# LSTM cell, step size and its product moved to GpSimd, and four buffers for the products with B, in a Mamba stage

## The reference

```python
dt = softplus(einsum('blr,cr->blc', dt_in, dw) + db)      # the step size
def step(h, inp):
    dA = exp(dt_t[..., None] * A)
    h = dA * h + (dt_t * u_t)[..., None] * B_t[:, None, :]
    y = einsum('bcn,bn->bc', h, C_t)
# the LSTM, each direction, 33 time steps of 64 sequences, 64 hidden units
g = xt @ wih.T + h @ whh.T + bih + bhh
i, f, gg, o = split(g, 4)
c = sigmoid(f) * c + sigmoid(i) * tanh(gg)
h = sigmoid(o) * tanh(c)
```

## Time and profile before

| What | Value |
|---|---|
| median of 3 runs | 2159.1 us (2152.12 to 2165.97) |
| profiled execution | span 2159.5 us from its first to its last instruction; it has no other time of its own |
| busy in the span | PE 1857.5, DVE 1645.7, ACT 1298.3, POOL 1011.2 us |
| Mamba and LSTM stage | first scan at 46.3 us, last product with C at 836 us |
| idle time of GpSimd before products with B | 203.4 us over the kernel |
| a load of B, 429 KB | 4.6 us from issue to landing |

### The profile page before, as it was taken

How to read it: one execution, slowest core, us unless ns; L and a number is a source line. 1 busy time by engine, 2 the same in 40 slices (tenths; PEclk the granted TensorE clock), 3 DMA queues, 4 the chain that set the end, 5 groups by cost and what they waited for, 6 DMA issues and landing times. The chain is left out here.

```text
span 2159.5 us, 49411 instructions
## 1 busy us (share of the span) xinstructions
PE 1857.5 (86%) x19547; PEld 1357.8 (63%) x19547; DVE 1645.7 (76%) x2609; ACT 1298.3 (60%) x2660; POOL 1011.2 (47%) x775
## 2 busy tenths in 40 slices
PE   7888888889888867897878878889788699999999
PEld 4444444444443323444568877767676599999999
DVE  4999999999999996678465442346554589999897
ACT  5777777777776645114345444252456388888886
POOL 1777777777777773110017777300440033333333
PEclk9999999999999999899679999898899699999999
DMA  3544444444444442520038889501730411112000
GB/s 130 167 132 132 126 137 132 132 132 127 128 139 140 132 137 55 126 45 1 7 100 236 258 257 256 139 1 73 231 114 12 187 64 64 65 65 69 14 7 7
DMA packets 98037, 241.63 MB, mean 112 GB/s; under 512 B 15024, under 2 KB 48320, under 8 KB 95504
## 3 DMA queue, kind: packets, MB, share of 16 engines
q1 hardware_dynamic: 89120, 218.12, 32.7%
q0 software_dynamic: 7680, 15.74, 3.2%
q10 hardware_dynamic: 1008, 4.62, 0.6%
HBM read 226.25 MB, written 12.19 MB: 110 GB/s over the span
## 5 line engine op out<-in xcount | busy, mean ns | idle before, releaser
L1119 POOL TENSOR_TENSOR dBu<-du,Bs 128x858 f32<-128x858 f32 (+1 forms) x240 | 588.2, 2452 | 203.4 <-DVE hst L1046 94.6
L574 PE MATMUL py<-hst,ident 128*128 128x429 f32 (+1 forms) x960 | 416.7, 565 | 95.9 <-DVE hst L1056 95.1
L1046 DVE TENSOR_TENSOR_SCAN hst<-dA,dBu 128x858 f32<-128x858 f32 (+1 forms) x240 | 457.8, 1908 | 17.1 <-ACT dA L889 13.7
L889 ACT ACTIVATE dA<-dt,negA 128x416 f32<-128x416 f32 (+1 forms) x480 | 269.5, 596 | 177.2 <-DVE hst L1046 175.6
L574 PEld LDWEIGHTS py<-hst,ident 128*128 128x128 f32 x960 | 183.6, 202 | 292.3 <-DVE hst L1056 169.0
L3444 POOL TENSOR_TENSOR hm<-h,mw 128x264 f32<-128x264 f32 x128 | 89.7, 701 | 391.0 <-DVE h L3424 391.0
L1056 DVE TENSOR_TENSOR hst<-hst,Cs 128x858 f32<-128x858 f32 (+1 forms) x240 | 246.5, 1027 | 0.0
L3315 PE MATMUL pg<-hs,wh 128*128 128x66 f16 x6144 | 218.8, 194 | 4.8 <-issue 4.7
L3315 PE MATMUL pg<-xm,wi 128*128 128x66 f16 x6144 | 214.6, 195 | 6.8 <-issue 5.4
L3315 PEld LDWEIGHTS pg<-hs,wh 128*128 128x128 f16 x6144 | 204.8, 98 | 8.6 <-issue 5.1
L3315 PEld LDWEIGHTS pg<-xm,wi 128*128 128x128 f16 x6144 | 202.0, 98 | 11.3 <-issue 5.9
(11 more groups left out here) (568 smaller groups left out, 3458.8 us busy)
## 6 DMA issues: line engine op xcount, KB each, us to landing
wb<-sf_w SPq DMA_DIRECT2D x96, 514.0 KB, 4.9
Bs<-bc_rows SPq DMA_DIRECT2D x96, 429.0 KB, 4.6
Cs<-bc_rows SPq DMA_DIRECT2D x96, 429.0 KB, 3.5
mw<-route_weights SPq DMA_DIRECT2D x8, 2112.0 KB, 10.1
wb<-gf_w SPq DMA_DIRECT2D x24, 514.0 KB, 4.9
Bs<-bc_rows SPq DMA_DIRECT2D x24, 396.0 KB, 5.0
Cs<-bc_rows SPq DMA_DIRECT2D x24, 396.0 KB, 4.6
mb<-route_masks SPq DMA_DIRECT2D x8, 1088.0 KB, 5.8
```

What stands on the lines that cost most here:

```text
L574: return nc.tensor.matmul(out, weight, moving, **kw)
L889: last = a(o, by_seq(dt[:, j % 2, h, 0:n])[:, :, 1:S], ACT.Exp, scale=negA[:, l, h * DST + k:h * DST + k + 1])
L1046: v.tensor_tensor_scan(hst[:, g % HR, 0:2 * n], dA[:, g % 2, 0:2 * n], dBu[:, g % 2, 0:2 * n], 0.0, ALU.mult, ALU.add).then_inc(h_ready, 1)
L1119: g_.tensor_tensor(dBu[:, g % 2, 0:2 * n].rearrange("p (a n) -> p a n", a=2), du[:, j % 2, :, 0:n], Bs[:, q % NBS, k % BG, 0:n].unsqueeze( ...
```

## The change

- The LSTM's sigmoids are now made whole: behind the four tanh ScalarE writes (tanh + 1)/2 of three gates from PSUM into an SBUF tile in one more instruction. The halves folded into the recurrent and fusion weights go away, with the two copies that applied them.
- `lstm_c` moves from VectorE to GpSimd, as one product of 128 columns and one sum of 64, issued behind the product with B of k = 3, 7, 11; `lstm_h` moves too, one product of 64 columns behind k = 4, 8, 12.
- The step size and its product with the inputs (dt, du) move to GpSimd, behind k = 11 and 13, for all chunks but the first.
- dBu has four buffers in place of two, so GpSimd waits for the scan of group g-4.
- The hold at k = 10 is gone.

```diff
+DR = 4
-        dBu = sb("dBu", [128, 2, 2 * SCW])
+        dBu = sb("dBu", [128, DR, 2 * SCW])
...
+        gates = sb("gates", [128, 3, NB])
+        gc = sb("gc", [128, 2, NB])
+        prod = sb("prod", [128, 2, NB])
...
 # ScalarE, lstm_gates
                 for g in range(3):
-                    a(act3[:, g, :], pre[:, g, :], ACT.Tanh, scale=0.5, bias=lb[:, 2, g:g + 1])
-                a(cz[:, 0, :], pre[:, 3, :], ACT.Tanh, bias=lb[:, 0, 3:4]).then_inc(gated, 1)
+                    last = a(act3[:, g, :], pre[:, g, :], ACT.Tanh, scale=0.5, bias=lb[:, 2, g:g + 1])
+                last.then_inc(tanhed, 1)
+                a(gc[:, 0, :], pre[:, 3, :], ACT.Tanh, bias=lb[:, 0, 3:4])
+                act.wait_ge(tanhed, t + 1)
+                a(gates[:, :, :], act3, ACT.Identity, scale=0.5, bias=half[:, :]).then_inc(gated, 1)
...
-            a(whh[:, :, :, :], whh[:, :, :, :], ACT.Copy, scale=0.5).then_inc(lw_ready, 1)
-            a(fw[:, 1, :], fw[:, 1, :], ACT.Copy, scale=0.5).then_inc(lw_ready, 1)
...
 # VectorE: in soften only for the first chunk, else gone
-                v.tensor_tensor(dt[:, j % 2, :, 0:n], pos[:, :, 0:n], ln[:, :, 0:n], ALU.add).then_inc(dt_done, 1)
-                v.tensor_tensor(du[:, j % 2, :, 0:n], dt[:, j % 2, :, 0:n], u[:, j % 2, :, 0:n], ALU.mult).then_inc(du_done, 1)
...
 # VectorE: the three instructions of lstm_c and the one of lstm_h are gone
 # GpSimd
+            def lstm_c(t):
+                pool.wait_ge(gated, t + 1)
+                if t >= 1:
+                    pool.wait_ge(c_ready, t)
+                else:
+                    pool.wait_ge(c_zeroed, 1)
+                g_.tensor_tensor(prod[:, :, :], gates[:, 0:2, :], gc[:, :, :], ALU.mult).then_inc(prods_ready, 1)
+                pool.wait_ge(prods_ready, t + 1)
+                if t >= 1:
+                    pool.wait_ge(tc_ready, t)
+                g_.tensor_tensor(gc[:, 1, :], prod[:, 0, :], prod[:, 1, :], ALU.add).then_inc(c_ready, 1)
+            def lstm_h(t):
+                pool.wait_ge(tc_ready, t + 1)
+                if t >= 2:
+                    pool.wait_ge(hs_kept, t - 1)
+                g_.tensor_tensor(hr[:, t % 2, :], gates[:, 2, :], tc[:, :], ALU.mult).then_inc(r_ready, 1)
+            def step_size(j):
+                pool.wait_ge(patched, j + 1)
+                pool.wait_ge(d_read, 2 * j + 2)
+                g_.tensor_tensor(dt[:, j % 2, :, 0:n], pos[:, :, 0:n], ln[:, :, 0:n], ALU.add).then_inc(dt_done, 1)
+            def step_inputs(j):
+                pool.wait_ge(dt_done, j + 1)
+                pool.wait_ge(u_gated, j + 1)
+                g_.tensor_tensor(du[:, j % 2, :, 0:n], dt[:, j % 2, :, 0:n], u[:, j % 2, :, 0:n], ALU.mult).then_inc(du_done, 1)
...
-                if k == 10:
-                    if j + 1 < NI:
-                        pool.wait_ge(du_done, j + 2)
-                    if j >= 2:
-                        pool.wait_ge(m_scaled, j - 1)
...
-                if g >= 2:
-                    pool.wait_ge(h_ready, g - 1)
+                if g >= DR:
+                    pool.wait_ge(h_ready, g - DR + 1)
...
+                if j < LSTM_ITEMS and k in (3, 7, 11):
+                    lstm_c(PER_ITEM * j + (k - 3) // 4)
+                if j < LSTM_ITEMS and k in (4, 8, 12):
+                    lstm_h(PER_ITEM * j + (k - 4) // 4)
+                if j + 1 < NI and k == 11:
+                    step_size(j + 1)
+                if j + 1 < NI and k == 13:
+                    step_inputs(j + 1)
```

More of the change, by code:

```diff
@@ L476, in mamba_lstm @@
         fb = sb("fb", [128, 1])
-        cz = sb("cz", [128, 2, NB])
-        ig = sb("ig", [128, NB])
+        half = sb("half", [128, 1])
+        gates = sb("gates", [128, 3, NB])
+        gc = sb("gc", [128, 2, NB])
+        prod = sb("prod", [128, 2, NB])
         tc = sb("tc", [128, NB])
@@ L499, in mamba_lstm @@
             stage(nc, "wop_ready wop_kept cent_ready cent_kept sq_ready var_ready var_kept var_logged rstd_ready m_scaled m_done"))
-        (diag_ready, bias_set, lw_ready, gates_ready, gated, prods_ready, c_ready, tc_ready, r_ready, hs_kept, fused, fused_added) = ctx.enter_context(
-            stage(nc, "diag_ready bias_set lw_ready gates_ready gated prods_ready c_ready tc_ready r_ready hs_kept fused fused_added"))
+        (diag_ready, bias_set, lw_ready, gates_ready, half_set, c_zeroed, tanhed, gated, prods_ready, c_ready, tc_ready, r_ready, hs_kept, fused, fused_added) = ctx.enter_context(
+            stage(nc, "diag_ready bias_set lw_ready gates_ready half_set c_zeroed tanhed gated prods_ready c_ready tc_ready r_ready hs_kept fused fused_added"))
         b_loaded = ctx.enter_context(stage(nc, " ".join(f"b_loaded{k}" for k in range(NBS))))
@@ L865, in lstm_gates @@
                 for g in range(3):
-                    a(act3[:, g, :], pre[:, g, :], ACT.Tanh, scale=0.5, bias=lb[:, 2, g:g + 1])
-                a(cz[:, 0, :], pre[:, 3, :], ACT.Tanh, bias=lb[:, 0, 3:4]).then_inc(gated, 1)
+                    last = a(act3[:, g, :], pre[:, g, :], ACT.Tanh, scale=0.5, bias=lb[:, 2, g:g + 1])
[3 more added lines that the diff above has]
+                a(gates[:, :, :], act3, ACT.Identity, scale=0.5, bias=half[:, :]).then_inc(gated, 1)
             def lstm_cell(t):
                 act.wait_ge(c_ready, t + 1)
-                a(tc[:, :], cz[:, 1, :], ACT.Tanh, scale=0.5).then_inc(tc_ready, 1)
+                a(tc[:, :], gc[:, 1, :], ACT.Tanh).then_inc(tc_ready, 1)
             def lstm_keep(t):
@@ L920, in _ @@
             decay(2)
-            act.wait_ge(lw_ready, 3)
+            act.wait_ge(lw_ready, 1)
+            act.wait_ge(half_set, 1)
             lstm_gates(0)
@@ L988, in soften, with first_step @@
                 v.copy_predicated(ln[:, :, 0:n], small[:, :, 0:n], t).then_inc(patched, 1)
-                dve.wait_ge(patched, j + 1)
-                dve.wait_ge(d_read, 2 * j + 2)
-                v.tensor_tensor(dt[:, j % 2, :, 0:n], pos[:, :, 0:n], ln[:, :, 0:n], ALU.add).then_inc(dt_done, 1)
-                dve.wait_ge(dt_done, j + 1)
-                dve.wait_ge(u_gated, j + 1)
-                if j >= 2:
-                    dve.wait_ge(dBu_ready, DST * (j - 1))
-                v.tensor_tensor(du[:, j % 2, :, 0:n], dt[:, j % 2, :, 0:n], u[:, j % 2, :, 0:n], ALU.mult).then_inc(du_done, 1)
+                if j == 0:
+                    first_step()
+            def first_step():
+                l, at, n = item(0)
+                dve.wait_ge(patched, 1)
+                dve.wait_ge(d_read, 2)
+                v.tensor_tensor(dt[:, 0, :, 0:n], pos[:, :, 0:n], ln[:, :, 0:n], ALU.add).then_inc(dt_done, 1)
+                dve.wait_ge(dt_done, 1)
+                dve.wait_ge(u_gated, 1)
+                v.tensor_tensor(du[:, 0, :, 0:n], dt[:, 0, :, 0:n], u[:, 0, :, 0:n], ALU.mult).then_inc(du_done, 1)
             def gate(j):
@@ L1011, in back @@
                                        op0=ALU.mult, op1=ALU.mult).then_inc(m_scaled, 1)
[L1013 to L1031, removed]
             def fuse(c):
@@ L1045, in scan @@
                 dve.wait_ge(dA_ready, g + 1)
-                v.tensor_tensor_scan(hst[:, g % HR, 0:2 * n], dA[:, g % 2, 0:2 * n], dBu[:, g % 2, 0:2 * n], 0.0, ALU.mult,
+                v.tensor_tensor_scan(hst[:, g % HR, 0:2 * n], dA[:, g % 2, 0:2 * n], dBu[:, g % DR, 0:2 * n], 0.0, ALU.mult,
                                      ALU.add).then_inc(h_ready, 1)
@@ L1064, in _ @@
                     weigh(g - 1)
[L1065 to L1069, removed]
                 if j >= 1 and k == 1:
@@ L1096, in build @@
                 g_.tensor_tensor(wt[:, l % 2, r, :], W(l, "wi", 0, DIN), cw[:, r, :], ALU.mult).then_inc(built, 1)
+            def lstm_c(t):
[15 more added lines that the diff above has]
+            def step_size(j):
+                l, at, n = item(j)
+                pool.wait_ge(patched, j + 1)
+                pool.wait_ge(d_read, 2 * j + 2)
+                g_.tensor_tensor(dt[:, j % 2, :, 0:n], pos[:, :, 0:n], ln[:, :, 0:n], ALU.add).then_inc(dt_done, 1)
+            def step_inputs(j):
+                l, at, n = item(j)
+                pool.wait_ge(dt_done, j + 1)
+                pool.wait_ge(u_gated, j + 1)
+                g_.tensor_tensor(du[:, j % 2, :, 0:n], dt[:, j % 2, :, 0:n], u[:, j % 2, :, 0:n], ALU.mult).then_inc(du_done, 1)
             g_.memset(edge[:, 0:1], SER_B)
             g_.memset(edge[:, 1:2], 4000.0 / 32).then_inc(edge_set, 1)
+            g_.memset(half[:, :], 0.5).then_inc(half_set, 1)
+            g_.memset(gc[:, 1, :], 0.0).then_inc(c_zeroed, 1)
             g_.memset(whh[:, :, :, :], 0.0).then_inc(l_zeroed, 1)
```

5 lines of the change are left out of this document (1 added, 4 removed).

## The result

The changed kernel takes 2182.4 us (median of 4 runs, 2180.1 to 2185.1) against 2161.9 us (4 runs of before): ratio 1.010, 95% interval 1.0076 to 1.0125. That is 20 us slower; forecast were 2195 us and slower. The profiled execution has a span of 2178.2 us.

The account below looks back on a forecast made before the run. VectorE was taken as the bound. Delays of 7.8 us less 4.1 us removed work and 0.7 us hidden waits gave +3.0 us a chunk, times 11, plus 2 us: 2159.5 + 35 = 2195 us, range 2123 to 2222 us.

Parts of the forecast that it names:

- The exclusion: A weigh (VectorE's product with C) starting during a GpSimd instruction is late by what is left of it, less 0.12 us.
- The removed work: Per LSTM chunk VectorE loses step size and its product, 2.06 us, and three time steps, 2.0 us: 4.1 us.
- The delays: Late weighs on VectorE per LSTM chunk, from moved large operations, regained products and small operations: 7.8 us.
- The term of the moved dt and du: Two large GpSimd operations a chunk, each delaying a weigh by some 1.4 us: +2.8 us a chunk.
- regained products: GpSimd loses lead waiting for gates twice an LSTM chunk; each product regained delays a weigh 1.4 us: +2.8 us.
- nine small operations: Moved LSTM operations on GpSimd push products across weighs or stand before one: +2.2 us a chunk (0 to 3.9).
- The three chunks without LSTM: Chunks behind the LSTM ones that still make a next step size: 2.8 - 2.06 = +0.7 us each.
- The last chunk: Final chunk of the stage, which has none of the moved work: 0.
- Edits at nothing: Added Identity, removed weight copies, earlier loads of B and removing the hold alone were each put at no cost.
- shared time is enough: Rival: both sides' SBUF access, 51.6 us an LSTM chunk, fits below today's 53.6; faster, 2131 us; chance 0.17.
- Half of the delays: Rival: GpSimd never regains its lead, 2.8 + 1.2 us of delays against 4.1 us; no change, 2159 us; chance 0.20.
- ScalarE's queue: Rival: tanh waiting for the cell update holds back decay factors, 1 us in 33 steps; 2228 us; chance 0.07.

Follow-up runs that it names:

- psum_before: Kernel before, with the weigh multiplying by decay factors in PSUM instead of C in SBUF: 2174.7 us, ratio 1.0046 to the kernel before.
- psum_after: Changed kernel, with the weigh multiplying by decay factors in PSUM instead of C in SBUF: 2132.6 us, ratio 0.9848 to the kernel before.
- after_pairs: Changed kernel with VectorE doing two scans, then two weighs, and the gate one group later: ratio 1.0608 to the kernel before.
- step_only: Kernel before with four buffers, no hold, and only dt and du on GpSimd: ratio 1.0041 to the kernel before.
- lstm_only: Changed kernel with dt and du back on VectorE, only the LSTM's cell on GpSimd: ratio 1.0133 to the kernel before.
- lstm_hold: lstm_only with the hold put back: ratio 1.0245 to the kernel before.
- after_three: Changed kernel with three buffers, and GpSimd waiting for ln before the product with B of k = 11: ratio 1.0034 to the kernel before.
- buf_nohold: Kernel before with four buffers and without the hold, nothing moved to GpSimd: ratio 1.0106 to the kernel before.
- after_two: Changed kernel with two buffers in place of four: ratio 1.0311 to the kernel before.
- lock_du: Kernel before with only du moved to GpSimd and GpSimd operations locked to places meeting no two-SBUF-operand VectorE instruction: 2204.9 us, ratio 0.9953 to the kernel before.

## Why the prediction was right, and where its size was off

**What bounds the stage**, VectorE, held: it is busy 802.6 of 814.8 us, and 610.2 us in the 11 LSTM chunks hold 600.2 us of its work.

**The exclusion**, read from three rows with at most 0.65 us left, held up to 1.91 us left, three times as far, with the same constant. psum_before and psum_after show it from the other side. The Trainium skill, "SBUF — State Buffer", section on the two separate sides, says that such a VectorE operation and a GpSimd operation exclude each other for the whole instruction, and the traces agree; that the waiting side goes next when both queue (ser at 682.66, the pairs of after_pairs) I show here from the rows.

**The removed work**, 4.1 us an LSTM chunk, is as foreseen: 571.7 us of VectorE's busy time before, less 11 x 4.1, plus 11 x 6.7 us of measured delays (below) are 600.3 us, and 600.2 are measured. The idle time before scans fell by 0.6 us a chunk (14.9 to 8.5 us over 11 chunks; 0.7 foreseen).

**The delays were mis-sized**: 7.8 us a chunk foreseen. Measured are (1431 - 1032) ns x 16 = 6.4 us of late weighs, from the group rows of the two LSTM windows, and 0.3 us on the softening operations, 6.7 us. Net 6.7 - 4.1 - 0.6 = +2.0 us a chunk in place of +3.0 (the two windows give 1.85). The term of the moved dt and du held: step_only has 2.9 us a chunk more of late weighs (41 us in 14 chunks), 2.8 foreseen, though most of it falls on products with B that run late behind them: dt and du themselves stand beside only 10 late weighs of the changed kernel, for 11.7 us. The terms that were too large together are the two of the LSTM, regained products and nine small operations, 2.8 + 2.2 = 5.0 us: of the 6.7 us, 3.8 are left for them. lstm_only has as much in late weighs, 3.8 us an LSTM chunk more than before, but late du and ser beside them. The small operations are the likelier part of the excess. They stand beside late weighs only 8 times in 33 time steps, for 1.1 us in the whole kernel, and are shorter than my line gave (0.45 us, 0.32 and 0.32, 1.1 us a time step). But they can also push a product across a weigh, and the trace does not tell such a product from a regained one, so how the 3.8 us divide between the two terms stays open.

**That regained products cost is shown**: lstm_hold pays 3.5 us a chunk for two of them with no moved work in that chunk. after_three, with one less to regain, gains 14 us, 1.3 us in each of 11 chunks (foreseen 1.4 a product), which fits but has the second edit in it. The single delay reaches 1.8 us, for a product of 858 columns that starts free lasts 1.7 to 2.0 us (1.86 us on average in psum_before); my 1.64 us is the time of one that starts behind a weigh. So each was dearer and there were fewer: 41 weighs above 2.0 us in 11 chunks, up to 2.82 us, where I had foreseen four or five a chunk of up to 2.6 us.

**The three chunks without LSTM** came to 52.4 us in place of 51.7: +0.7 us, as foreseen. **The last chunk**, put at 0, is 1.3 us longer (47.1 us in place of 45.8), and there the missing hold is seen at work, on m:

```profile
838.42 2.44 POOL L1127 TENSOR_TENSOR dBu<-du,Bs 128x792 f32<-128x792 f32 x1 [0.28 <-DVE hst L1032]
839.08 2.25 DVE L1016 SCALAR_TENSOR_TENSOR m<-cent,w,rstd 128x429 f32<-128x429 f32 x1
```

The same m takes 0.65 us in the kernel before.

**Edits at nothing.** "Removing the hold alone gives nothing" was wrong: with full lead it costs 23 us (buf_nohold). The forecast suffered little, because in the changed kernel GpSimd mostly stands in a wait for gates or for ln when the softening begins: ser is at 1178 ns in the LSTM chunks, 0.15 us late on average, and that is one ser of 2.70 us out of 11. The missing hold shows again in the last chunk, above. The added Identity and the loads of B cost nothing that shows (0.7 us of waits for B).

**The rivals.** That shared time is enough fails at the time left unused: 610.2 us of LSTM chunks against 51.6 x 11 = 568. Half of the delays had 4.0 us a chunk; 6.7 are measured. ScalarE's queue is no part of the changed kernel (its tanh waits 2.7 us in all) but is real where GpSimd has less lead: 34.8 us in lstm_hold, 61.3 us in after_two.

In the sum, the stage is 23.9 us longer (11 x 1.85, 3 x 0.73 and 1.3), where 35 us were foreseen; the device time is 20.5 us longer, and the span of the two profiled executions 18.7 us. In these two, what follows the stage is 6 us shorter (1316.4 in place of 1322.5 us) and what lies ahead of it 0.9 us longer; why is open.

## What to carry to other kernels

Before moving an elementwise operation from VectorE to GpSimd, find which VectorE operations read two SBUF operands and count the time that both sides need the access, not the busy share: here GpSimd was idle for a quarter of the stage, and lock_du found room for one operation of 1.6 us a chunk. Work that fits must also be placed. lock_du lets a GpSimd operation be released by an event at the start of a VectorE operation that it has to wait for anyway, and lets GpSimd catch up beside VectorE operations with a PSUM operand; which of the two matters more was not tested. More buffers take such a lock away; a lead lost in a wait is bought back at VectorE's cost.

## What the runs showed that I had not expected

- Two VectorE operations in a row, each with two SBUF operands, are no block: a GpSimd operation that waits gets its turn between them. ser took 2.67 us in place of 1.03 in all 14 chunks of buf_nohold, and a pair of weighs 3.60 us in place of 1.9.
- A GpSimd product of 858 columns lasts 1.56 to 1.72 us behind a weigh that it had to wait for, and 1.86 us on average (192 of them) where no weigh excludes it (psum_before, the product beside a weigh with one operand in PSUM and beside the scan), as if part of its start were hidden in the wait; that reason is not shown.
- Moving one part more made it faster: lstm_only has a ratio of 1.0133, the changed kernel, with dt and du on GpSimd too, 1.010. In lstm_only du is late in most chunks and stands on VectorE (2.03 us), where the changed kernel has none of it, and ser is late in the three chunks without LSTM (2.5 to 2.9 us), where in the changed kernel it is on time (1.0 us): there the moved step size waits for ln and holds GpSimd back.
